# A decoder layer on one core: the chosen rows of its third stage fetched and written back by indexed DMA, with the steps in a new order

## The reference, cut to what matters

```python
scores = x @ w_router
_, idx = jax.lax.top_k(scores, CAP)                       # CAP = 128 of 256 tokens
x_sel = jnp.take_along_axis(x, idx[:, :, None], axis=1)
h = rmsnorm(x_sel, g1)
...                                                        # attention with 16 heads over the 128 chosen rows
x_attn = o @ W_out.T
h2 = rmsnorm(x_sel + x_attn, g2)
x_ff = jax.nn.silu(h2 @ W1.T) * (h2 @ W2.T) @ W3.T
out = x.at[jnp.arange(Bq)[:, None], idx].set(x_sel + x_attn + x_ff)
```

## Time and profile before

| what | value |
|---|---|
| median of three runs | 952.1 us (951.48 to 952.46) |
| span of the profiled execution, first to last instruction | 947.8 us |
| busy: PE, DVE, ACT, POOL | 883.4, 727.6, 595.2, 218.6 us |
| instructions | 21833 |
| mean granted TensorE clock | 0.995 |

### The profile page before, as it was taken

How to read it: one execution, slowest core, us unless ns; L and a number is a source line. 1 busy time by engine, 2 the same in 40 slices (tenths; PEclk the granted TensorE clock), 3 DMA queues, 4 the chain that set the end, 5 groups by cost and what they waited for, 6 DMA issues and landing times.

```text
span 947.8 us, 21833 instructions
## 1 busy us (share of the span) xinstructions
PE 883.4 (93%) x7652; PEld 750.3 (79%) x7652; DVE 727.6 (77%) x1670; ACT 595.2 (63%) x1582; POOL 218.6 (23%) x379
## 2 busy tenths in 40 slices
PE   7888999999999999999999999999999999998987
PEld 4657797978879797887979788787979788786855
DVE  4878878787887878888787879788787878866342
ACT  4365757667574767657575766757576675745533
...
DMA packets 20465, 25.05 MB, mean 26 GB/s; under 512 B 1488, under 2 KB 18000, under 8 KB 20432
## 3 DMA queue, kind: packets, MB, share of 16 engines
...
## 4 chain that ended last, share of the span: by engine, by line
PE 64%; DVE 20%; ACT 7%; issue 7%; DMA 1%; POOL 0%; DVEq 0%; SPq 0%; ACTq 0%; POOLq 0%
PE bank L1064 21%; PE bank L1370 4%; PE bank L1166 4%; PE bank L1356 4%; PE bank L1331 3%; PE bank L1245 3%; PE bank L1253 3%; PE bank L1424 2%; DVE before L950 2%; ACT L615 2%; PE bank L1319 2%; PE bank L1184 2%; PE bank L1457 2%; PE bank L1080 2%; DVE prob L850 2%
## 5 line engine op out<-in xcount | busy, mean ns | idle before, releaser
L652 ACT ACTIVATE w_raw_or_stage_c<-bank,c_nmax 128x128 f32<-128x128 f32 x256 | 90.6, 375 | 12.3 <-DVE c_nmax L981 12.3
L615 ACT ACTIVATE prob<-bank,b_folded 128x256 f32<-128x256 f32 x128 | 53.7, 471 | 46.0 <-PE bank L1064 45.8
L981 DVE TENSOR_REDUCE c_nmax<-bank 128x4 f32<-128x512 f32 x64 | 43.5, 683 | 48.1 <-PE bank L1356 48.1
L809 DVE TENSOR_TENSOR a_s<-bank,const 128x512 f32<-128x512 f32 x112 | 71.8, 677 | 9.0 <-PE bank L1166 6.4
L729 DVE TENSOR_TENSOR b_s_lo<-prob,b_s_hi 128x512 fp32r<-128x512 f32 x64 | 54.2, 848 | 27.3 <-ACT b_s_hi L503 27.3
L426 POOL TENSOR_TENSOR a_tr_lo<-a_norm,a_tr_hi 128x512 fp32r<-128x512 f32 x16 | 21.0, 1310 | 216.9 <-ACT a_tr_hi L503 216.9
L402 POOL TENSOR_TENSOR x<-x,vectors_by_row 128x512 f32<-128x512 f32 x16 | 20.7, 1292 | 161.7 <-DVE w_raw_or_stage_c L975 161.7
L652 ACT ACTIVATION_READ_ACCUMULATOR w_raw_or_stage_c<-bank,c_nmax 128x1 f32 x256 | 55.1, 215 | 0.0
L799 DVE RECIPROCAL a_e<-a_e 128x512 f32<-128x512 f32 x16 | 53.4, 3340 | 0.0
L1064 PE MATMUL bank<-b_s_hi,w_mlp_hi 128*128 128x256 f32 x256 | 44.8, 298 | 4.8 <-ACT prob L615 4.6
L1475 PE MATMUL bank<-ones_bf 128*128 128x512 bf16 x164 | 46.7, 410 | 1.0 <-POOL ones_bf L400 1.0
...
## 6 DMA issues: line engine op xcount, KB each, us to landing
x_in<-in_x SPq DMA_DIRECT2D x16, 256.0 KB, 2.7
qc<-in_ctx SPq DMA_DIRECT2D x16, 256.0 KB, 3.2
b_f<-in_ctx_t SPq DMA_DIRECT2D x16, 256.0 KB, 3.4
out<-w_raw_or_stage_c SPq DMA_DIRECT2D x16, 256.0 KB, 2.1
...
```

The lines of the kernel that those rows point to most:

```text
L615: act_in(prob[:, 2 * (j % 2) + n, :], b0[:, n * T:(n + 1) * T], ACT.Gelu, bias=b1p[:, f:f + 1]).then_inc(b_gelu.sem, 1)
L652: act_in(c_e[g % 2][:, j * R:(j + 1) * R], (c1, c2)[g % 2][:, j * R:(j + 1) * R], ACT.Exp, bias=c_nmax[:, n:n + 1], accum_out=c_den[:, hea ...
L809: tt(heads(A_MASKED[t][n][:, :]), heads(A_SCORES[n][:, :]), tri.unsqueeze(1).broadcast_to([P, 4, P]), ALU.mult).then_inc(a_scput.sem, 1)
L981: nc.vector.tensor_reduce(c_nmax[:, 4 * g:4 * g + 4], heads((c1, c2)[g % 2][:, :]), axis=AX.X, op=ALU.max, negate=True).then_inc(c_max.sem, 1)
```

## The change

Chosen rows are now moved by DMA. The normed rows, x2 and the RMS factor of each token stand side by side in one tile (`rows`); SP writes it to a table in DRAM (`store_rows`, 256 rows of 513 numbers, 2052 bytes each). The rank of each token comes from two comparisons with a sum over the row (`c_rank`, now on DVE), which read the transposed scores in bank b0 of stage b. `c_sel` makes one one-hot matrix in bf16; two products of one column each (`c_idx`) turn it into the index of the row that has each rank, `c_idxput` writes it as an integer, and POOL fetches the 128 rows with an indexed DMA (`c_pick`). `c_hsc` scales them, and `c_ht` is two transposes. `c_h2put` moves from ACT to DVE and adds the chosen rows to the projection. `c_ob` moves to POOL and is the plain sum for all tokens; SP stores it, and after that store POOL overwrites the chosen rows with an indexed DMA (`c_put`) at indices kept by `c_keep`. `c_hx` (POOL) adds the x2 of the chosen rows. `c_before`, `c_selu`, `c_yhi`, `c_ylo`, `c_scat` and `c_done` are gone. ACT names the table set that has both exp and ln before `a_qout`. ORDER is a new list and starts at another point of the round; its loop runs rounds 5 to 15, since `c_put++` makes the pipeline one round deeper. SP's list has `next_x` last. WARM_AT is empty. The 14 products at the start stay. In the diff a removed function stands with its first line alone.

```diff
-a_y+ c_w2 c_att+ b_up_1+ b_down_0+ b_up_2+ c_dput+ b_gelu_1+ a_yhi+ b_ghi_1+ a_mean c_o+ b_glo_1+ c_w3 c_w0
-b_gelu_2+ a_done+ c_xo+ c_h2put+ c_h2lo+ b_mean b_ghi_2+ c_h2hi+ b_gelu_3+ a_proj+ b_glo_2+ a_normed b_ghi_3+
-c_w4 c_h2tp+ b_glo_3+ c_gate_0+ b_normed b_kept+ b_o+ b_omean+ c_gate_1+ b_fb2+ a_kept+ b_frstd+ b_up_3+
-b_down_1+ c_gu_0+ a_ylo+ c_h2rms+ c_gtlo_0+ a_rstd b_onormed+ b_down_2+ b_down_3+ c_gu_1+ b_tanhk b_rstd
-c_tanh_0+ b_qb c_tanh_1+ c_gu_2+ c_gthi_0+ c_gtp_0+ c_gtp_1+ c_ff_0+ a_tp b_done+ c_gthi_1+ a_thi c_gtlo_1+
-c_mean a_tlo c_y+ b_tanhq c_ff_1+ b_v b_pnorm c_ylo+ c_yhi+ b_vput c_normed a_q c_scat+ a_k a_qout c_sbc
-c_done+ b_orstd+ c_rscore a_kout b_diff c_before a_val c_rank b_log b_dtp a_ktp a_phi_q a_phi_k c_sel a_vput
-c_hput b_vq c_ht b_rtp b_ratio c_qk c_selu a_csum b_sid c_score_0 b_dput a_kput a_kq c_ob c_max_0 b_rput
-a_mask a_sput c_qkput b_sexp a_state c_exp_0 c_max_1 b_fput c_w5 a_dput b_fmean a_scput_0 a_scput_1 a_den b_fd
-c_v c_exp_1 c_vput c_w6 c_etput_0 a_scput_2 a_score_0 c_etp_0 c_score_1 a_scput_3 c_w7 c_w1 c_etp_1 c_max_2
-c_etput_1 a_score_1 b_htp b_fnormed a_att_0 c_etp_2 c_exp_2 c_w8 a_scput_4 b_hhi c_max_3 b_hlo c_rstd c_rms1
-a_scput_5 a_scput_6 c_dinv b_up_0 a_scput_7 c_exp_3 c_etput_2 c_etp_3 a_dinv c_dtp c_dbc c_etput_3 b_glo_0
-b_gelu_0 b_ghi_0 c_w9 a_att_1
+c_w2 c_exp_2+ b_up_0+ a_scput_5+ c_etp_3+ c_dtp+ c_dinv+ a_att_1+ b_hhi+ a_scput_6+ c_exp_3+ a_scput_7+
+c_etput_2+ b_up_1+ a_dinv+ b_glo_0+ c_put++ c_dbc+ a_y+ c_att+ c_w3 b_gelu_0+ b_ghi_0+ c_keep+ a_mean
+c_etput_3+ b_glo_1+ a_kept+ c_o+ b_gelu_1+ b_down_0+ a_done+ b_glo_2+ b_up_2+ a_yhi+ a_proj+ a_normed c_xo+
+c_h2put+ b_ghi_1+ a_ylo+ b_mean b_up_3+ c_dput+ b_gelu_2+ b_ghi_2+ c_h2sq+ b_gelu_3+ b_down_1+ c_h2tp+
+b_down_2+ c_h2lo+ c_h2hi+ b_ghi_3+ b_glo_3+ a_rstd b_down_3+ c_w0 b_tanhk c_w4 a_thi c_h2rms+ b_tanhq b_normed
+a_tp b_vput c_gu_0+ b_o+ b_omean+ c_tanh_0+ a_tlo b_onormed+ b_v b_done+ a_q b_rstd a_k c_gu_1+ c_mean b_pnorm
+b_orstd+ c_gate_0+ c_gu_2+ c_normed c_tanh_1+ c_gtp_0+ a_qout c_rscore b_log b_diff c_gthi_0+ c_sbc c_rstd
+c_rank a_kout c_sel c_gate_1+ c_rms1 c_idxput a_val c_idx b_vq c_gtp_1+ b_dtp c_gthi_1+ c_gtlo_0+ b_ratio
+c_hx+ c_ff_0+ b_dput b_rtp b_rput a_phi_q c_gtlo_1+ a_phi_k c_y+ c_hsc c_ff_1+ b_sid a_csum c_ht b_qb a_kq
+c_pick c_w5 c_hput a_vput a_kput a_ktp a_sput c_qk b_sexp c_max_0 c_w6 c_ob c_qkput c_max_1 b_fput a_mask
+a_state a_dput b_kept c_exp_0 c_w7 b_fmean a_scput_0 c_exp_1 b_fb2 a_den c_score_0 b_fd a_scput_1 c_v
+a_scput_2 a_scput_3 c_max_2 a_score_0 b_fnormed c_w1 c_w8 c_etp_0 c_vput c_etput_0 c_score_1 c_etp_1 a_scput_4
+a_score_1 b_frstd b_htp a_att_0 c_max_3 c_etp_2 c_etput_1 b_hlo c_w9
...
-WARM_AT = {(0, "a_q"): 2, (0, "a_ktp"): 1, (0, "a_state"): 2, (0, "a_score_0"): 1, (0, "a_score_1"): 1, (0,
...
+WARM_AT = {}
...
+        rows = sb("norm_x2_rms", [P, TT, 2 * D + 4])
+        c_norm, x2 = rows[:, :, 0:D], rows[:, :, D:2 * D]
...
+        y_out = parts[0][:, 0:D]
+        c_hx = parts[0][:, D:2 * D]
...
-        before = sb("before", [P, 3 * T], BF16)
-        sel_t = sb("select_by_rank", [P, T], F32R)
-        sel = sb("select_by_token", [P, TT, R])
-        sel_s = sb("select_scaled", [P, TT, R])
+        sel = sb("select_by_token", [P, TT, R], BF16)
+        index = sb("row_of_slot", [P, 1], mybir.dt.uint32)
+        index_out = sb("row_of_slot_out", [P, 1], mybir.dt.uint32)
+        batch_at = sb("first_row", [P, 1])
+        picked = sb("picked_rows", [P, 2 * D + 4])
+        x_sel, x2_sel, r1_sel = picked[:, 0:D], picked[:, D:2 * D], picked[:, 2 * D:W]
...
+            def store_rows(b):
+                sp.wait_ge(*c_normed(b))
+                sp.sem_inc(passed.sem, 1)
+                sp.wait_ge(*c_rms1(b))
+                sp.sem_inc(passed.sem, 1)
+                if not first(b):
+                    sp.wait_ge(*picked_in(b - 1))
+                    sp.sem_inc(passed.sem, 1)
+                sp.dma_start(token_rows_by_p, rows[:, :, 0:W]).then_inc(rows_out.sem, 16)
...
+            with sp.Fori(2, B - 1) as i:
+                next_ctx(i - 1)
+                store_rows(i - 2)
+                store(i - 2)
+                next_ctx_t(i - 1)
                 next_x(i)
...
+                    pool.wait_ge(*rows_out(b - 1))
...
-                    pool.wait_ge(*c_sels(b - 1))
-                nc.gpsimd.tensor_tensor(c_r1[:, :], c_ms[:, :], C["minus_half"], ALU.pow).then_inc(c_rms1.sem, 1)
+                    pool.wait_ge(*rows_out(b - 1))
+                nc.gpsimd.tensor_tensor(c_r1, c_ms[:, :], C["minus_half"], ALU.pow).then_inc(c_rms1.sem, 1)
+
+            def c_ob_(b):
+                pool.wait_ge(*c_normed(b))
+                if not first(b):
+                    pool.wait_ge(*out_done(b - 1))
+                nc.gpsimd.tensor_tensor(ob[:, :, :], x2, c_norm, ALU.add).then_inc(c_ob.sem, 1)
+
+            def c_pick_(b):
+                pool.wait_ge(*c_idxput(b))
+                pool.wait_ge(*rows_out(b))
+                if not first(b):
+                    pool.wait_ge(*c_hx_s(b - 1))
+                    pool.wait_ge(*c_h2put(b - 1))
+                pool.sem_inc(passed.sem, 1)
+                nc.gpsimd.indirect_dma_start(
+                    picked[:, 0:W], None, token_rows[:, :], bass.IndirectOffsetOnAxis(ap=index[:, 0:1], axis=0)) \
+                    .then_inc(picked_in.sem, 16)
+
+            def c_hx_(b):
+                pool.wait_ge(*c_h2put(b))
+                pool.wait_ge(*picked_in(b))
+                if not first(b):
+                    pool.wait_ge(*c_y(b - 1))
+                nc.gpsimd.tensor_tensor(c_hx, c_h2[:, :], x2_sel, ALU.add).then_inc(c_hx_s.sem, 1)
+
+            def c_put_(b):
+                pool.wait_ge(*c_y(b))
+                pool.wait_ge(*c_kept(b))
+                pool.wait_ge(*out_done(b))
+                pool.sem_inc(passed.sem, 1)
+                nc.gpsimd.indirect_dma_start(
+                    out[:, :], bass.IndirectOffsetOnAxis(ap=index_out[:, 0:1], axis=0), y_out, None) \
+                    .then_inc(y_stored.sem, 16)
...
+                nc.scalar.preload_act_table_set("natural_log_exp_and_others")
...
-            def c_h2put_(b):
...
+            def c_h2sq_(b):
+                act_e.wait_ge(*c_h2put(b))
+                act_in(flat(c_hT[:, :, :]), c_h2[:, :], ACT.Square, scale=1.0 / D ** 0.5, accum_out=c_sq2[:, :]) \
+                    .then_inc(c_h2sq.sem, 1)
...
-                    dve.wait_ge(*c_xo(b - 1))
                     dve.wait_ge(*c_ob(b - 1))
+                    dve.wait_ge(*rows_out(b - 1))
...
-            def c_before_(b):
+            def c_rank_(b):
                 dve.wait_ge(*c_sbc(b))
-                earlier, later = tie_mask[:, 0, :], tie_mask[:, 1, :]
...
+                for t in range(TT):
+                    if t:
+                        dve.wait_ge(*c_rank(b, t))
+                    stt(tie[:, :], b0[:, 0:T], c_sc[:, t:t + 1], tie_bound[:, t, :], ALU.subtract, ALU.is_gt,
+                        accum_out=c_rk[:, t:t + 1]).then_inc(c_rank.sem, 1)
 
             def c_sel_(b):
-                dve.wait_ge(*c_rank(b))
-                nc.vector.tensor_copy(c_rk[:, :], c1[:, T:T + TT]).then_inc(c_rkput.sem, 1)
-                dve.wait_ge(*c_rkput(b))
-                dve.wait_ge(*c_rms1(b))
+                if not first(b):
+                    dve.wait_ge(*c_idx(b - 1))
                 for t in range(TT):
-                    ts(sel_s[:, t, :], C["iota_row"], c_rk[:, t:t + 1], c_r1[:, t:t + 1], ALU.is_equal, ALU.mult) \
-                        .then_inc(c_sels.sem, 1)
-
-            def c_selu_(b):
...
-            def c_ob_(b):
...
+                    dve.wait_ge(*c_rank(b, t + 1))
+                    ts(sel[:, t, :], iota_bf[:, :], c_rk[:, t:t + 1], None, ALU.is_equal).then_inc(c_sel.sem, 1)
+
+            def c_idxput_(b):
+                dve.wait_ge(*c_idx(b))
+                if not first(b):
+                    dve.wait_ge(*picked_in(b - 1))
+                nc.vector.tensor_copy(index[:, :], b0[:, T:T + 1]).then_inc(c_idxput.sem, 1)
+
+            def c_hsc_(b):
+                dve.wait_ge(*picked_in(b))
+                ts(c_h[:, :], x_sel, r1_sel, None, ALU.mult).then_inc(c_hsc.sem, 1)
+
+            def c_keep_(b):
+                if not first(b):
+                    dve.wait_ge(*y_stored(b - 1))
+                    dve.wait_ge(*c_next(b - 1))
+                ts(index_out[:, :], index[:, :], batch_at[:, 0:1], None, ALU.add).then_inc(c_kept.sem, 1)
+                dve.wait_ge(*c_kept(b))
+                ts(batch_at[:, :], batch_at[:, :], float(T), None, ALU.add).then_inc(c_next.sem, 1)
...
+            def c_h2put_(b):
+                dve.wait_ge(*c_xo(b))
+                tt(c_h2[:, :], c2[:, 0:D], x_sel, ALU.add).then_inc(c_h2put.sem, 1)
...
-                dve.wait_ge(*c_h2put(b))
-                tt(c_h2[:, :], c1[:, 0:D], c_h2[:, :], ALU.add).then_inc(c_y.sem, 1)
-
-            def c_ylo_(b):
...
```

(30 more changed lines are left out.)

150 lines of the change are left out of this document (46 added, 104 removed).

## The result

The changed kernel takes 972.6 us (median of 4 executions, 971.1 to 974.1), beside 952.3 for the kernel before on the same chip: a ratio of 1.022, with a 95% interval of 1.020 to 1.023. The prediction was 915.7 us, 892 to 941. It is slower, by 20 us.

The account below looks back on a forecast made before the run. PE was taken to bound the kernel, busy 51.84 of each 54.39 us round. The span 947.8 - 15 x 2.89 + 7 = 911.4 us, plus 4.3 from span to median, gave 915.7 us, range 892 to 941.

Parts of the forecast that it names:

- Net 2.89 us less: PE products per round: 3.16 us removed, two transposes (0.22) and two one-column products (0.05) added.
- equal to the 0.6 that goes: PE's new waits, for c_sel and c_idxput, cost the 0.6 us a round of the removed ranking and gather waits.
- DVE "at nothing": DVE loses 15 instructions a row and gets 9 small ones; costed at nothing, with 10 us of slack per round.
- POOL's moved additions at nothing: POOL's queued additions, each big one 1.3 us, got no cost in the sum; POOL is busy a quarter of the round.
- The slower rival: POOL cannot write the fetch while DVE runs; 33 us more, 985 us; chance 0.08.
- Store 4.2, fetch 4.0, cover 5: Table store 4.2 us, indexed fetch 4.0, hidden behind some 5 us of other work, with 1 us to spare.
- the fetch is seen in part: Rival: store and fetch each 1 us slower, 1.6 us of each round comes back; 940 us; chance 0.13.
- only outside the DVE stretch: Rival: PE's saving counts only where DVE does not set the pace, 0.86 us a round; 946 us; chance 0.05.
- ACT's tables at nothing: ACT's four table loads of 1.28 us a round become two; pays nothing in the loop.
- The ramps at +7: Filling and emptying the pipeline, 131.9 us before, changes by -9 + 14 + 2 = +7 us.
- -9 + 14: Ramps without the 150 filler products: 9 us of their own time saved, 14 us lost to PE's lower clock.
- The fetch's +2: Ramps: the fetch has no cover in the last rounds; net 2 us for both ramps, between 0 and 8.

Follow-up runs that it names:

- pool_both: Changed kernel with both edits of POOL's queue: c_hx and b_qb earlier, behind b_rstd; c_ob later, waiting for a_kq two rows behind; 947.7 us.
- rstd_no_fetch_wait: pool_both with b_rstd ahead of c_h2rms on POOL, and c_hsc not reading the fetched rows (attention over wrong tokens); 930.3 us.
- b_rstd's place: Edit to pool_both that puts b_rstd ahead of c_h2rms in POOL's order; alone on pool_both it takes 938.4 us.

## Why the prediction was wrong

- **"Net 2.89 us less" on PE.** Right in kind, off in size: 2.24 (51.84 to 49.60). The prices were pieces of the chain of waits. In a round of the changed kernel the two transposes are busy 0.38 us, not 0.22, and `c_idx` 0.20, not 0.05. That is 0.31 of the 0.65 between 2.89 and 2.24; the rest was not traced to a product.
- **PE's waits "equal to the 0.6 that goes".** Wrong: 5.3 us a round in place of 2.5. With both edits of POOL's queue 3.4.
- **DVE "at nothing".** Its work did fall, to 42.5 us a round once nothing holds it. In the changed kernel it is 45.7, by the hold. The count was off: some 4 instructions a row went (1670 to 1609 in all), not the 6 that 15 less 9 makes.
- **POOL's moved additions at nothing: the sum has no term for them, and the only reason given is "POOL's additions run beside a busy DVE at the same 1.3 us". This is the step that failed.** The row quoted for it, POOL's addition from 428.68 to 429.97, lies beside an idle DVE, which waited 2.26 us for PE until 430.85 (first line below). And it is POOL's duration, where the price stands in DVE's. It was to be seen in the trace of before, at one place (DVE's timeline, last line below): `b_s_lo` took 1.37 us where POOL's `a_ylo` ran from 450.13 to 451.42, against 0.69 for the others. POOL's other additions lay beside idle time or instructions with a bank or one tile. The change moves `c_hx`, `b_qb`, `c_ob` and `b_kept` beside `c_normed`, `c_rscore` and `a_phi`, in the 16.8 us where I had myself found DVE at 16.2. Price: 2.0 us a round by pool_both, and 25 us of the whole (972.6 to 947.7).

```profile
430.85 0.69 DVE L981 TENSOR_REDUCE c_nmax<-bank 128x4 f32<-128x512 f32 x1 [2.26 <-PE bank L1356]
...
447.66 0.69 DVE L729 TENSOR_TENSOR b_s_lo<-prob,b_s_hi 128x512 fp32r<-128x512 f32 x1 [0.53 <-ACT b_s_hi L503]
...
450.61 1.37 DVE L729 TENSOR_TENSOR b_s_lo<-prob,b_s_hi 128x512 fp32r<-128x512 f32 x1 [0.25 <-ACT b_s_hi L503]
```

- **The slower rival** had the two engines shutting each other out, but the wrong way: I let DVE block POOL's descriptors. They were written in 1.10 us; POOL's plain additions block DVE. Its 985 us was near the result by chance, not by its mechanism (and its sum has 9 for the ramps where the others have 7).
- **Store 4.2, fetch 4.0, cover 5.** Store 4.3; fetch 3.5 from the start of POOL's instruction, but that starts 0.8 to 1.0 us after POOL could go on, and in pool_both the store lands 0.7 us after the index is there, which the prediction did not ask. In the changed kernel no wait, as forecast, but only because DVE was late. Without the hold store and fetch cost 0.65 us a round. That is the rival "the fetch is seen in part" at less than half of its 1.6.
- **The rival "only outside the DVE stretch"** has 946 us, near pool_both's 947.7, but by chance: without the hold the round gained 1.43 us (54.39 to 52.96), not 0.86, and the ramps are longer than it had them.
- **ACT's tables at nothing.** Right: two loads more change no round. Over the whole kernel the difference, 950.2 to 947.7, is within their spreads (944.2 to 950.3, and 945.2 to 952.0).
- **The ramps at +7.** They grew by 15. The fillers' removal, "-9 + 14", measured +15.5 in the old kernel and +9.6 in the changed one. With the 9 us of the prediction for the fillers' own time, which no run checks, the low clock costs about 24 us in the one and 19 in the other, not 14. I had taken 9 of 30 us in the sparse rounds at the end; the clock was at 0.56 to 0.59 in 40 us of it. By the rule of the Trainium skill (TensorE: Matmul & The Clock Gate, part 1) that loss was 30; both kernels lie between, and the changed one, which the forecast is about, nearer to 14. The fetch's +2 was too small as well: taking its wait away gave 7 to 10 us in pool_both's ramps.
- **The range** reached to 941, for I gave the hold no case at all: 0.90 on faster rested on POOL's steps being free. (The inner range's upper end, 936, is also less than its own parts give, 21 for the round and 13 for the ramps.) Of the two signs of being wrong the round's came, 54.94 against 53; the ramps grew by 15, under their 20.

The steady round, put together from the runs: rstd_no_fetch_wait takes 52.15 us; + 0.16 for b_rstd's place (52.31), + 0.65 for store and fetch (52.96), + 1.98 for the hold gives 54.94. These are differences of measured rounds, so that they add is no test, and in another order the shares differ (b_rstd's place was worth 0.47 with the fetch's wait in). 54.39 - 2.24 gives 52.15 too, in part by chance: PE is busy 49.30 us in that run's round, 2.54 less than before, and idle 0.35 more.

With the same shares the miss of 56.9 us (972.6 less 915.7) comes to this: 15 rounds of 3.44 us more than forecast are 51.6, of which the hold is 29.7, PE's work and waits 9.8, store and fetch 9.8 and b_rstd's place 2.4. The ramps add 8.2 (15.2 for 7), and 2.9 go, since the median is 1.4 us above the profiled span here, not 4.3. The 15 us of the ramps are fillers and fetch together with the new order; how much is the order alone was not tried.
